# The bias of the first expert layer moved from TensorE to DVE, in the tail of a MetaFormer block

## The chip, the cores and the metric

The kernel runs on one core of one Trainium2 chip. The metric is the device time of one execution in microseconds, as the median of several runs. The engines are named as in the profile: PE (TensorE), DVE (VectorE), ACT (ScalarE), POOL (GpSimd) and SP (SyncE). Each has its own queue of instructions, worked off in order, and the engines meet only through semaphores.

## The reference, cut to what matters

The input is x of 16 batches x 128 x 128 x 128 in float32. A channel attention block with its normalisations comes first. Then follows a layer of 64 experts in which each expert picks its own 8 tokens of each batch:

```python
probs = softmax(t_normed @ gate_w.T + gate_b, axis=tokens)
vals, idx = top_k(probs, 8)                     # per batch and expert
pooled = einsum('bked,bke->bed', x[idx], vals)  # 16 batches x 64 experts x 128
h = gelu(concat(pooled, 1) @ weight1)           # weight1[e]: 129 x 512, row 128 is the bias
out = concat(h, 1) @ weight2                    # weight2[e]: 513 x 128, row 512 is the bias
outputs.at[idx].add(out * vals)                 # scattered back to the picked tokens
```

## The kernel before, in words

The long first part of the kernel streams the 16 batches through all engines: normalise, Gram matrix, attention, output norm, store to `out`, logits, top 8. It is not touched. What follows it, from about 1951 us of the profiled execution to the end, is the tail: the expert layer. Its 64 experts are worked in 16 groups of 4 (`NG`), and 4 groups make a quarter (`Q`). A loop over `SLOTS` = 23 slots, written out in the same way for PE, ACT and DVE, is a software pipeline: in slot t

- PE runs `layer1(t)`, then `turn2(t-3)`, `outputs(t-7)`, `turn1(t-1)`, `codes(t-6)`, `layer2(t-2)` and `combine(t-7)`. When t is a multiple of 4, `pooling(t//4, 1)` comes ahead of `layer1`, and one slot before that `pooling(.., 0)` comes behind it.
- ACT runs `pooled` (line 621, when t is a multiple of 4), the GELU of group t (L632), the copy of the second layer's result of group t-2 (L637), `scales` (L612 and L615, in slots 1, 2, 5, 6, 9, 10), and the copy of the combined rows of t-7 (L645) into one of four buffers `C`.
- DVE runs the copy `OT` of group t-3 (L1127), the product `V` of t-7 (L1135), the copy `HTs` of t-1 (L1141), `equal(t-6)` (L1100 to L1112), and in slots 1, 2, 5, 6, 9, 10 `prepare` (L1078 to L1091), which waits in its middle for the `scales` of ACT and ends with `FW`, the operand of `pooling`.
- POOL scatters: for each of the 16 groups u, once `C` of u and the indices `idxs` of u are there, four indirect DMAs (L490) add the rows to `out`.

GELU and the two functions of `scales` need different activation tables, so ACT loads a table before each change of function.

`layer1(g)` computes the first layer of 4 experts into one PSUM bank `O[g % 2]` of 128 x 512. Expert i of the group has the partitions 32i to 32i+31, and its 16 batches are the first 16 of them. `biases` (L773) first writes the bias to all 32 partitions: for each expert a product of a column of the identity, broadcast to 32, with the 64 x 512 tile `b1s` of all biases. Then the product of `PT` (16 batches) with the weights (L786) is added to it in PSUM. `layer2` (L804) does the same with 128 columns and `b2s`. A product in the profile is two records, so `biases` of one group is 8 of them.

`PT` is written by `pooled`, once per quarter, from a PSUM bank in the order batch, expert into the order expert, batch. SP issues the weight loads: 8 of 256 KB for each group. The loads of group g, from g = 6 on, wait until `layer2(g-6)` is done.

The tiles of the tail lie over those of the first part: `half` is the odd half of `U`, `spare` is `zT`. ACT's GELU reads PSUM and writes `Hs`, of which there are two.

## Time and profile before

| | us |
|---|---|
| median of 3 runs | 2142.67 (2136.2 to 2142.91) |
| the profiled execution | 2155.56 |
| its span, first to last instruction | 2153.8 |
| granted PE clock, mean over the span | 0.957 |

The profiled execution is 12.9 us (0.6%) over the median of the runs. Its times are used for durations, and differences worked out in it are applied to the median. The engines are all 85% to 90% busy over the span, but this is the first part's doing; the tail has to be read by itself.

### The profile page before, as it was taken

How to read it: one execution, taken by the hardware profiler on the slowest of the kernel's cores; microseconds unless marked ns; L12 is line 12 of the kernel's file. 1: busy time of each engine (PE TensorE's matmuls, PEld its weight loads, DVE VectorE, ACT ScalarE, POOL GpSimd, SP SyncE). 2: the span in 40 equal slices, each digit the busy share in tenths (PEclk: the TensorE clock that was granted, in tenths of full speed). 3: DMA queues.
4: the chain of work that ended last, by engine and by line, in shares of the span. 5: the costliest groups of instructions: out<-in, count | busy, mean ns of one | idle time of the engine just before them, and what ended most of it. 6: DMA issues, size and time to landing. Idle time of an engine off the chain costs nothing.

```text
span 2153.8 us, 42420 instructions
## 1 busy us (share of the span) xinstructions
PE 1873.0 (87%) x11917; PEld 1286.6 (60%) x11917; DVE 1822.8 (85%) x4612; ACT 1882.0 (87%) x5020; POOL 1939.2 (90%) x2068
## 2 busy tenths in 40 slices
PE   6999999999999999999999999999999987636991
PEld 6866666666666666666666666666666643213570
DVE  4689999999999898989899999999999899624670
ACT  6899999999999999999999999999999987743420
POOL 5799999999999999999999999999999999961387
PEclk9999999999999999999999999999999998765995
DMA  5498888887888888888788888888788676694963
GB/s 188 157 262 222 228 223 206 226 229 216 218 218 235 224 227 210 224 231 222 215 216 231 229 224 220 212 229 227 213 222 223 178 182 162 165 263 124 282 104 32
DMA packets 111068, 447.92 MB, mean 208 GB/s; under 512 B 10575, under 2 KB 52404, under 8 KB 61684
## 3 DMA queue, kind: packets, MB, share of 16 engines
q1 hardware_dynamic: 81140, 302.61, 42.9%
q0 software_dynamic: 29696, 142.61, 34.2%
q8 instruction: 98, 1.61, 0.3%
q14 instruction: 134, 1.10, 0.1%
HBM read 306.78 MB, written 138.41 MB: 207 GB/s over the span
## 4 chain that ended last, share of the span: by engine, by line
ACT 38%; POOL 21%; issue 17%; PE 16%; DVE 5%; ACTq 1%; DMA 1%; POOLq 0%; SPq 0%; DVEq 0%
ACT U L553 16%; POOL U L430 8%; POOL U L435 7%; ACT zT L516 6%; ACT UT L510 6%; PE G L747 4%; ACT LTS L580 3%; ACT LTS L525 3%; PE T L729 3%; PE O L680 2%; POOL zn L451 2%; POOL out_dram L490 2%; PE T L736 1%; ACT zn L574 1%; POOL U L442 1%
## 5 line engine op out<-in xcount | busy, mean ns | idle before, releaser
L553 ACT ACTIVATE U<-xa,nA,rA 128x128 f32<-128x128 f32 x1948 | 803.7, 483 | 2.1 <-issue 1.3
L747 PEld LDWEIGHTS G<-UT 128*128 128x128 f32 x4096 | 536.8, 192 | 226.5 <-issue 225.3
L430 POOL TENSOR_TENSOR U<-U,bet 128x512 f32<-128x512 f32 x512 | 651.4, 1272 | 2.2
L435 POOL TENSOR_TENSOR U<-U,rO 128x512 f32<-128x512 f32 x512 | 532.2, 1040 | 20.3 <-ACT rO L533 19.3
L747 PE MATMUL G<-UT 128*128 128x128 f32 x4096 | 542.0, 275 | 0.0
L680 PE MATMUL O<-U,MT 128*128 128x512 f32 x1024 | 529.5, 599 | 3.0 <-DVE U L938 3.0
L451 POOL TENSOR_TENSOR zn<-U,rZ 128x512 f32<-128x512 f32 x414 | 446.6, 1079 | 11.0 <-ACT rZ L564 10.3
L936 DVE BATCH_NORM_STATS2 stO<-O 128x6 f32<-128x256 f32 x1024 | 386.8, 423 | 50.2 <-PE O L680 49.5
L729 PE MATMUL T<-ident,U 128*128 128x128 f32 x2048 | 324.3, 281 | 119.1 <-ACT UT L510 108.6
L729 PEld LDWEIGHTS T<-ident,U 128*128 128x128 f32 x2048 | 224.6, 142 | 318.1 <-issue 314.1
L954 DVE BATCH_NORM_STATS2 stA<-xa 128x6 f32<-128x256 f32 x1024 | 386.8, 426 | 31.8 <-DMA xa<-in_x 28.5
L1033 DVE BATCH_NORM_STATS2 stZ<-U 128x6 f32<-128x256 f32 x1024 | 387.4, 424 | 31.1 <-DMA U<-in_x 31.0
L736 PE MATMUL T<-ident,zn 128*128 128x128 f32 x2048 | 322.1, 281 | 75.3 <-ACT zT L516 45.1
L938 DVE TENSOR_TENSOR U<-O,gam 128x512 f32<-128x512 f32 x512 | 348.3, 680 | 0.0
L516 ACT ACTIVATE zT<-T 128x512 f32<-128x512 f32 x512 | 297.6, 581 | 34.0 <-PE T L736 15.1
L736 PEld LDWEIGHTS T<-ident,zn 128*128 128x128 f32 x2048 | 235.6, 143 | 133.0 <-issue 115.0
L510 ACT ACTIVATE UT<-T 128x512 f32<-128x512 f32 x512 | 296.0, 578 | 10.5 <-PE T L729 8.9
L722 PE MATMUL LT<-zT,gwT 128*64 128x512 f32 x1024 | 284.9, 635 | 1.3 <-ACT LTS L525 1.3
L490 POOL DMA_INDIRECT out_dram<-U,UT x64 | 102.2, 1597 | 84.2 <-DVE UT L1112 59.6
L1044 DVE MAX8 CD<-LTS 128x8 f32<-128x2048 f32 x64 | 146.1, 2283 | 35.2 <-issue 35.2
L680 PEld LDWEIGHTS O<-U,MT 128*128 128x128 f32 x1024 | 156.1, 193 | 3.6 <-DVE U L938 3.6
L525 ACT ACTIVATE LTS<-LT 128x512 f32<-128x512 f32 x256 | 150.3, 587 | 2.2 <-issue 2.2
(151 smaller groups left out, 1655.0 us busy)
## 6 DMA issues: line engine op xcount, KB each, us to landing
xa<-in_x SPq DMA_DIRECT2D x128, 1024.0 KB, 6.3
U<-in_x POOLq DMA_DIRECT2D x128, 1024.0 KB, 10.8
out_dram<-U SPq DMA_DIRECT2D x128, 1024.0 KB, 8.6
U<-in_L_ffn_weight SPq DMA_DIRECT2D x112, 256.0 KB
LTS<-in_L_ffn_weight SPq DMA_DIRECT2D x16, 256.0 KB
xa<-out_dram,UT POOLq DMA_INDIRECT x64
out_dram<-U,UT POOLq DMA_INDIRECT x64
zT<-in_L_ffn_weight SPq DMA_DIRECT2D x1, 128.0 KB
```

What stands on the lines that cost most here:

```text
L430: gp.tensor_tensor(rows(a, i), rows(a, i), bet_b, ALU.add).then_inc(S["gb"], 1)
L435: gp.tensor_tensor(rows(a, i), rows(a, i), rO[:, i // 2 % 2, i % 2 * TI:(i % 2 + 1) * TI].unsqueeze(2).to_broadcast([P, TI, W]), ALU.mult) ...
L451: gp.tensor_tensor(zn[:, i % 2, :].rearrange("p (h w) -> p h w", w=W), rows(a, i), rZ[:, k % 2, i % IC * TI:(i % IC + 1) * TI].unsqueeze(2 ...
L510: sc.activation(UT[:, (a[0] * NI + i) % 3, :], T0[:, :], ACT.Copy).then_inc(S["ut_ready"], 1)
L516: sc.activation(zT[:, (a[0] * NI + i) % 3, :], T1[:, :], ACT.Copy).then_inc(S["zt_ready"], 1)
L553: last = sc.activation(utile(a, i, j), xa[:, k % XR, h * W:(h + 1) * W], ACT.Identity, scale=rA[:, k % 2, h:h + 1], bias=nA[:, k % 2, h:h ...
L680: te.matmul(O[i % NO][:, :], MT[:, a[0] % 2, :], chunk(a, i // IC)[:, o:o + IW], start=True, stop=True).then_inc(S["my"], 1)
L729: last = te.transpose(T0[:, j * W:(j + 1) * W], utile(a, i, j), ident[:, :])
L736: last = te.transpose(T1[:, j * W:(j + 1) * W], zn[:, i % 2, j * W:(j + 1) * W], ident[:, :])
L747: last = te.matmul(G[:, 0:P], v, v, start=(i == 0 and j == 0), stop=(i == NI - 1 and j == TI - 1))
L936: last = ve.bn_stats(stO[:, i // 2 % 2, h:h + 2, :].rearrange("p n s -> p (n s)"), pair(O[i % NO], n))
L1033: last = ve.bn_stats(stZ[:, k % 2, j:j + 2, :].rearrange("p n s -> p (n s)"), pair(chunk(a, k), j // 2))
```

## The change

The first layer's bias no longer comes through PE. `b1s`, one 128 KB load by SP, is gone. ACT's queue issues the biases instead: `bias_rows(g)` is four DMAs for group g, each of which reads the 512 biases of one expert and writes them to the expert's 32 partitions of `B1[:, g % 2, :]` (64 KB written by each). `bias_rows(0)` and `(1)` are issued ahead of the slots, behind the wait for the last stores of the first part; `bias_rows(t + 2)` is issued in slot t, behind the GELU of t. DVE gets one instruction per slot, at the head of the slot: it adds `O[t % 2]` and `B1` into `Hs`. The GELU now works in place on `Hs`. `PT` holds each batch twice, so that the products of both layers write all 32 partitions of an expert: their stationary operand has 32 columns where it had 16. `FW` changes its place with no change of size. The wait of `layer1(g)` for the bank is now for DVE's addition of g-2, no longer for the GELU of g-2.

```diff
--- before.py
+++ after.py
@@ -168,10 +168,10 @@
         OUTs = over(spare, 2, W, at=at_t)
         OT = over(half, 2, NB, P, at=at_h)
         first = over(spare, 4, P, at=at_t)
-        b1s = over(spare, HID, at=at_t, parts=E)
+        B1 = over(half, 2, HID, at=at_h)
         b2s = over(spare, W, at=at_t, parts=E)
-        FW = over(half, 2, NB, EQN, at=at_h)
-        PT = over(half, 2, EQN, NB, at=at_h)
+        FW = over(spare, 2, NB, EQN, at=at_t)
+        PT = over(half, 2, EQN, 2 * NB, at=at_h)
         small, at_s = UT[:, :, :].rearrange("p a n -> p (a n)"), [0]
         picked = hot[:, :, :].rearrange("p a n -> p (a n)")
 
@@ -206,11 +206,11 @@
                  "z_bn z_ln z_r zn zn_act u_pool trz zt_ready lg lt_done seg_v seg_i seg_nm seg_exp "
                  "tick cand cross crossed xv t0 t1 t2 texp rsum tv").split()
         S = {n: sem("s_" + n) for n in names}
-        s_tail = sem("s_tail"); s_prep = sem("s_prep"); s_bias = sem("s_bias")
+        s_tail = sem("s_tail"); s_prep = sem("s_prep"); s_bias = sem("s_bias"); s_b1 = [sem(f"s_b1{i}") for i in range(2)]
         s_rows = [[sem(f"s_rows{q}_{h}") for h in range(2)] for q in range(Q)]
         s_sc = [sem(f"s_sc{i}") for i in range(4)]
         s_w = [sem(f"s_w{i}") for i in range(WR // 4)]
-        tnames = ("sel part cut code rowf idx codt codc row eq fst nf idxs rbn rvar rln rr wv cen fw pmm p_done "
+        tnames = ("hb sel part cut code rowf idx codt codc row eq fst nf idxs rbn rvar rln rr wv cen fw pmm p_done "
                   "h ge trh ht o ou tro ott xt v cmm c").split()
         R_ = {n: sem("r_" + n) for n in tnames}
 
@@ -349,7 +349,6 @@
                 weights(e)
 
             sp.wait_ge(S["lg"], NB * NI // 2)
-            sp.dma_start(b1s, w1[:, W, :]).then_inc(s_bias, 16)
             sp.dma_start(b2s, w2[:, HID, :]).then_inc(s_bias, 16)
             sp.wait_ge(S["seg_exp"], NB * NS)
             sp.wait_ge(S["seg_i"], NB * NS)
@@ -618,18 +617,33 @@
                 act.wait_ge(R_["pmm"], 2 * q + 2)
 
                 wait(act, R_["h"], 4 * (q - 1))
-                sc.activation(PT[:, q % 2, :, :].rearrange("p e n -> p n e"),
-                              T0[:, 0:NB * EQN].rearrange("p (n e) -> p n e", e=EQN), ACT.Copy).then_inc(R_["p_done"], 1)
-
+
+                sc.activation(PT[:, q % 2, :, :].rearrange("p e (r n) -> p r n e", n=NB),
+                              T0[:, 0:NB * EQN].rearrange("p (n e) -> p n e", e=EQN).unsqueeze(1).to_broadcast([P, 2, NB, EQN]),
+                              ACT.Copy).then_inc(R_["p_done"], 1)
+
+            def bias_rows(g):
+
+                for i in range(4):
+                    act.dma_start(B1[32 * i:32 * i + 32, g % 2, :],
+                                  w1[4 * g + i:4 * g + i + 1, W, :].to_broadcast([32, HID])).then_inc(s_b1[g % 2], 16)
+
+
+            for k in range(NK):
+                act.wait_ge(s_store[NK + k], 16 * (NB // 2))
+            bias_rows(0)
+            bias_rows(1)
             for h in range(2):
                 scales(0, h)
             for t in range(SLOTS):
                 if t < NG and t % 4 == 0:
                     pooled(t // 4)
                 if t < NG:
-                    act.wait_ge(R_["h"], t + 1)
-                    wait(act, R_["trh"], t - 1)
-                    sc.activation(Hs[:, t % 2, :], O[t % 2][:, :], ACT.Gelu).then_inc(R_["ge"], 1)
+                    act.wait_ge(R_["hb"], t + 1)
+                    sc.activation(Hs[:, t % 2, :], Hs[:, t % 2, :], ACT.Gelu).then_inc(R_["ge"], 1)
+                    if t + 2 < NG:
+
+                        bias_rows(t + 2)
                 if 0 <= t - 2 < NG:
                     g = t - 2
                     act.wait_ge(R_["o"], g + 1)
@@ -777,14 +791,13 @@
                 q = g // 4
                 if g % 4 == 0:
                     pe.wait_ge(R_["p_done"], q + 1)
-                wait(pe, R_["ge"], g - 1)
-                biases(O[g % 2], g, b1s)
+                wait(pe, R_["hb"], g - 1)
 
                 pe.wait_ge(s_w[g % (WR // 4)], 128 * (g // (WR // 4) + 1))
                 for i in range(4):
                     e = 4 * g + i
-                    last = te.matmul(O[g % 2][32 * i:32 * i + NB, :], PT[:, q % 2, e % EQN, :], wslot(e)[:, 0, 0:HID],
-                                     start=False, stop=True)
+                    last = te.matmul(O[g % 2][32 * i:32 * i + 32, :], PT[:, q % 2, e % EQN, :], wslot(e)[:, 0, 0:HID],
+                                     start=True, stop=True)
                 last.then_inc(R_["h"], 1)
 
             def turn1(g):
@@ -801,7 +814,7 @@
                 for c in range(HC):
                     for i in range(4):
                         e = 4 * g + i
-                        last = te.matmul(O[2][32 * i:32 * i + NB, 0:W], HTs[:, g % 2, c * P + 32 * i:c * P + 32 * i + NB],
+                        last = te.matmul(O[2][32 * i:32 * i + 32, 0:W], HTs[:, g % 2, c * P + 32 * i:c * P + 32 * i + 32],
                                          wslot(e)[:, 0, HID + c * W:HID + (c + 1) * W], start=False, stop=(c == HC - 1))
                 last.then_inc(R_["o"], 1)
 
@@ -837,7 +850,7 @@
                                      start=True, stop=True)
                 last.then_inc(R_["cmm"], 1)
 
-            pe.wait_ge(s_bias, 32)
+            pe.wait_ge(s_bias, 16)
             for t in range(SLOTS):
                 if t == 0:
                     pooling(0, 0)
@@ -1117,6 +1130,12 @@
             for h in range(2):
                 prepare(0, h)
             for t in range(SLOTS):
+                if t < NG:
+                    dve.wait_ge(R_["h"], t + 1)
+                    dve.wait_ge(s_b1[t % 2], 64 * (t // 2 + 1))
+
+                    wait(dve, R_["trh"], t - 1)
+                    ve.tensor_tensor(Hs[:, t % 2, :], O[t % 2][:, :], B1[:, t % 2, :], ALU.add).then_inc(R_["hb"], 1)
                 if 0 <= t - 3 < NG:
                     g = t - 3
                     q = g // 4
```

## Rows read from the trace of the kernel before

**Rows 1.** Page, busy time of each engine over the span

```profile
PE 1873.0 (87%) x11917; PEld 1286.6 (60%) x11917; DVE 1822.8 (85%) x4612; ACT 1882.0 (87%) x5020; POOL 1939.2 (90%) x2068
```

**Rows 2.** Stretches: start:end, length, busy by engine, PE clock, DMA share, GB/s

```profile
2100.00:2154.00 54.00, 5.52 (x26) 4.69 (x24) 3.86 (x9) 1.79 (x3) 39.63 (x26) 0.58 0.36 31
```

**Rows 3.** Timeline of POOL: start, us, line, operation, idle before it

```profile
2020.51 1.65 POOL L490 DMA_INDIRECT out_dram<-U,UT  x1 [59.63 <-DVE UT L1112]
...
2030.89 1.56 POOL L490 DMA_INDIRECT out_dram<-U,UT  x1 [3.11 <-ACT U L645]
...
2034.62 1.94 POOL L490 DMA_INDIRECT out_dram<-U,UT  x1 [0.30 <-issue]
...
2040.93 1.56 POOL L490 DMA_INDIRECT out_dram<-U,UT  x1 [2.51 <-ACT U L645]
...
2049.19 1.56 POOL L490 DMA_INDIRECT out_dram<-U,UT  x1 [0.64 <-issue]
...
2145.69 1.56 POOL L490 DMA_INDIRECT out_dram<-U,UT  x1 [0.31 <-issue]
```

**Rows 4.** Of line L490: duration ns min/median/max, first and last start

```profile
L490 POOL DMA_INDIRECT out_dram<-U,UT x64: 1557/1563/2067, 2020.5 to 2145.7; - x64
```

**Rows 5.** Timeline, PE: first layer's bias (L773) and product (L786)

```profile
1967.03 1.93 PE L773 MATMUL O<-zT,ident 64*32 64x512 f32 x8 [0.69 <-ACT U L621]
...
2054.24 1.06 PE L773 MATMUL O<-zT,ident 64*32 64x512 f32 x8 [0.69 <-ACT U L621]
...
2055.24 1.05 PE L786 MATMUL O<-U 128*16 128x512 f32 x8
```

**Rows 6.** Timeline, PE: second layer's bias behind DVE

```profile
1985.81 0.65 PE L773 MATMUL O<-zT,ident 64*32 64x128 f32 x8 [2.07 <-DVE U L1127]
...
2002.70 0.42 PE L773 MATMUL O<-zT,ident 64*32 64x128 f32 x8 [0.44 <-DVE U L1127]
...
2008.78 0.42 PE L773 MATMUL O<-zT,ident 64*32 64x128 f32 x8 [0.91 <-DVE U L1127]
...
2016.32 0.42 PE L773 MATMUL O<-zT,ident 64*32 64x128 f32 x8 [0.15 <-DVE U L1127]
```

**Rows 7.** Timeline, ACT: the pooled copy and the second layer's copy

```profile
1966.38 0.60 ACT L621 ACTIVATE U<-T 128x256 f32<-128x256 f32 x1 [5.02 <-PE T L767]
...
2028.46 0.28 ACT L637 ACTIVATE zT<-O 128x128 f32<-128x128 f32 x1 [4.30 <-PE O L804]
```

**Rows 8.** Timeline, ACT: scales of slot 9, the copy behind

```profile
2035.56 1.28 ACT L612 ACT_TABLE_LOAD   x1
...
2037.94 0.21 ACT L612 ACTIVATE UT<-UT 128x8 f32<-128x8 f32 x1 [1.10 <-issue]
...
2039.58 0.58 ACT L645 ACTIVATE U<-MB 128x512 f32<-128x512 f32 x1
```

**Rows 9.** Timeline, DVE in slot 9 and at the start of slot 10

```profile
2033.71 0.69 DVE L1100 TENSOR_TENSOR U<-G,UT 128x512 f32<-128x512 f32 x1
...
2034.43 0.69 DVE L1106 TENSOR_TENSOR zT<-U,zn 128x512 f32<-128x512 f32 x1
...
2036.16 1.41 DVE L1078 BATCH_NORM_STATS2 zn<-xa 128x6 f32<-128x256 f32 x4
...
2040.12 0.68 DVE L1127 COPY U<-O 128x512 f32<-128x512 f32 x1
```

**Rows 10.** Timeline, SP: issues of weight loads

```profile
2007.01 1.89 SPq L335 DMA_DIRECT2D U<-in_L_ffn_weight  x1
...
2029.31 0.50 SPq L335 DMA_DIRECT2D U<-in_L_ffn_weight  x1
```

**Rows 11.** Stretches of the tail, columns as in the second group

```profile
1966.00:1975.00 9.00, 8.31 (x37) 1.50 (x38) 0.00 (x0) 2.92 (x4) 0.00 (x0) 0.50 0.01 2
...
1985.00:1998.00 13.00, 11.48 (x85) 6.38 (x85) 2.37 (x5) 2.91 (x5) 0.00 (x0) 0.51 0.74 229
...
2010.00:2022.00 12.00, 11.16 (x129) 7.87 (x121) 8.85 (x20) 6.61 (x10) 1.49 (x1) 1.00 1.07 328
```

## The prediction

> **What bounds the kernel now.** I read the first part of the profile's page first: every engine is busy 85% to 90% of the span [rows 1]. That is the first part of the kernel, which the change leaves alone; only the tail can move. The stretches come next: in the last 54 us PE works 5.5, DVE 3.9, ACT 1.8 and POOL 39.6 us [rows 2]. So the end belongs to POOL's scatters. There are 64, of 1.56 us in the median and 0.30 between two, a pitch of 1.87 us [rows 4, 3]. From 2049.19 (first scatter of group u=3) to 2145.69 (the last) are 96.5 us for 51 pitches, 1.89 each: POOL never waits there. It waits only ahead of u=0 (2020.51), u=1 (idle 3.11), u=2 (2.51) and u=3 (0.64), the first for DVE's indices and the others for ACT's copy C [rows 3]. What PE, DVE and ACT do after slot 10 costs nothing: POOL needs 4 x 1.87 = 7.5 us a slot, and the others need less. The end is the latest of: readiness of u, plus 64-4u pitches. So the question is when u=0 to u=3 become ready, and those are made in slots 0 to 10, from 1966 to 2049.
>
> In these slots three chains take turns. In slots 1 to 3 and 5 to 7 it is DVE's prepare, which waits for ACT's scales and their table loads, and keeps PE's second layer waiting for the copy OT: four such waits, before 1985.81, 2002.70, 2008.78 and 2016.32 [rows 6]. In slots 4 and 8 PE itself with the pooled copy. In slots 9 and 10 DVE again: it begins prepare at 2036.16, leaves it at 2040.12 [rows 9], and C of u=2 stands on ACT's queue behind the scales that prepare feeds (2039.58) [rows 8].
>
> **The change part by part.** *PE's bias products go.* Eight records of L773 take 1.93 us at the low clock and 1.06 at the high one, against 1.05 for the product behind them; in a row that is 0.99 us of pitch at the high clock (2054.24 to 2055.24), 1.9 at the low one [rows 5]. The low clock (0.50 granted, 1.2 GHz) holds from 1966 to 1975 and again for nearly all of 1985 to 1998 [rows 11]. Removed: 16 times, of which groups 0, 1 and 4 at 1.9 and 2, 3, 5 to 10 at 1.0. Only where PE is what is late does it count: slots 0, 4, 8, 9.
>
> *DVE's addition comes.* It reads PSUM and SBUF over 128x512, as L1100 does: 0.69 us, about 0.6 from start to start [rows 9]. It stands at the head of DVE's slot, between the product and the GELU. So from the start of layer1 to the GELU 1.9 or 1.0 goes and 0.7 + 0.1 comes. In slots where DVE is late, 0.6 us is added whole.
>
> *The pooled copy doubles.* L621 takes 0.60 us for 256 elements written with a stride [rows 7]; L645 takes 0.58 for 512 contiguous ones [rows 8] and L637 0.28 for 128 [rows 7], which makes 0.17 fixed and 0.83 ns an element. So the strided write costs twice as much an element, and 512 of them cost 0.17 + 0.85 = 1.03 us; the ends are 0.60 (elements alone count) and 1.20 (all doubles). I take 1.03: +0.43 us in slots 0, 4 and 8, whole, as PE waits for it.
>
> *ACT issues four DMAs a slot.* No DMA is issued by ACT before. SP's issues take 0.50 us with quiet engines (2029.31) and up to 1.89 with full ones (2007.01) [rows 10]. The ends are 0 and 4 x 1.89 = 7.6 us a slot; I take four times 0.48, that is 1.9 us, because the quiet row is the kind met in most slots. The eight issues ahead of the slots fall into ACT's idle time before 1957.7 and cost nothing. The others stand between the GELU and the copy L637, where ACT mostly waits for layer2 anyway (4.30 us at 2028.46 [rows 7]): free in slots 4 and 7 to 10. In slots 1 and 2, where GELU and scales follow closely, they cost 1.9 us each.
>
> *The transfers.* 256 KB more a group beside 2 MB of weights; the DMA engines are full from 2010 to 2022 (share 1.07, 328 GB/s [rows 11]), so +12% there, about 0.8 us a group. Each bias has from the GELU of t to the product of t+2, at least 6 us (slot 0 to 2) and mostly 10 to 13. Nothing shown bounds the latency of a second hardware queue; I take it as hidden, with the cost of its failure among the rivals.
>
> *32 columns for 16, 32 rows written, FW's place, b1s gone:* the products stream the same 512 or 128 columns; the weight loads grow inside the pitch. Nothing, at most 0.1 us a slot, hidden behind POOL from slot 11 on.
>
> **The replay.** With these prices and the measured durations of all other instructions I walk the queues from 1966.38, keeping the clock as it was. Slot 0: PT ready +0.4; the product of group 0 ends at 1969.3 instead of 1970.8; GELU of 0 at 1970.1 (before 1970.9). Slots 1 and 2: DVE reaches prepare 3.3 us earlier; the first scales end 1.5 earlier (1977.9), as ACT issues DMAs first; the second scales, another 1.9 later, end at 1984.9 against 1984.5, and DVE now has two additions before its copy: layer2(1) starts at 1986.8 (before 1985.8), 1.0 late. Slot 4: +0.4 for PT, -1.9 for the bias: the product of group 4 ends at 1995.8 (before 1996.3). Slot 5: layer2(3) 2001.6 (2002.7), as the bias of group 5 is gone too. Slot 6: the addition of group 6 stands behind prepare: layer2(4) 2008.5 (2008.8). Slot 7: another addition: layer2(5) 2016.75 (2016.3). So the indices and C of u=0 come 0.45 late, first scatter 2020.95. Slot 8: +0.4 PT, -1.0 bias, and PE, not DVE, is late: C of u=1 ends 1.3 earlier, scatter 2029.6 (2030.9). Slot 9: a second bias gone, DVE enters prepare 2.0 earlier: scatter of u=2 2038.95 (2040.9). Slot 10: DVE is late from here, addition and prepare in a row: u=3 at 2047.9 (2049.2). From there POOL runs through as before. Sum: -1.3 us at u=3, and -1.3 at the end. The bound on the good side: with u=1 to 3 never waited for, POOL would win 0.3 to 5.4 us of gaps [rows 3] and lose the 0.45.
>
> One rule speaks to a term I set to nothing. The scatters of 1.94 us instead of 1.56 start 0.2 us after DVE's L1106, with two SBUF operands (2034.43 and 2034.62 [rows 9, 3]); beside L1100, with one in PSUM, none is long. The addition is of L1100's kind, so I charge nothing; were it of the other, up to 13 collisions of 0.38 us after u=3 would add 5 us. The Trainium skill, "SBUF — State Buffer", section "Who interferes with whom", says that a DVE instruction with two SBUF inputs blocks a GpSimd instruction that reads SBUF and one with at most one does not; by that rule, too, the addition costs POOL nothing, and the two rows fit it.
>
> **The rivals.** *R1, the issues on ACT are slow.* Where the DMA engines are full, SP's issues take twice the quiet time on average and up to 1.89 us. At 1.0 us each in slots 5 to 10, ACT's four take 4.0: scales of slot 5 +2.1, of slot 6 another +2.1, C of u=0 about +4; slots 8 to 10 hide part; u=3 3 to 7 us later than in my replay, so +2 to +6 us: 2144.5 to 2148.5. For it: row 2007.01. Against: these lengthen when SP's own backlog of several groups is long, and ACT has only 4 small transfers at a time. It decides from about 0.8 us an issue.
>
> *R2, the clock.* The change takes work out of PE in slots 1 to 8, and the low clock is already granted after gaps (idle of 2.07 us at 1985.81, then 0.51 over 1985 to 1998 [rows 6, 11]). If it stays low through slots 5 to 8 as well, each has some 3 us of PE work more, half of it on the chain: +6 us, less 1.3: +5, 2147.5. Against: after the change PE still works 7 of 10 us from 1987 to 1998.
>
> *R3, issues cost ACT nothing.* If an issue overlaps the running GELU and is short, slots 1 and 2 win back 3 us, and u=0 to u=3 follow: -4.3, 2138.4. This is the good end and still below 0.3%.
>
> *R4, biases land late.* If the second queue waits behind SP's backlog (2 groups, 4 MB at 328 GB/s, 13 us), DVE waits up to some 3 us in slots 7 to 9 with all its queue behind: +3 to +8 us, 2147. The Trainium skill, "DMA: Bandwidth & Descriptors", section "Queues, rings and completion order", says that each DMA engine goes round robin between its queues by packet; by that rule R4 is out, and no row here shows two hardware queues at once.
>
> *R5, nothing.* The gains and losses cancel, 0: inside the forecast's range.
>
> **How the numbers follow.** The forecast, -1.3 +- 3 us on the median, is 2142.67 - 1.3 = 2141.4. Chances: forecast with R5 0.58, R1 0.14, R2 0.08, R3 0.11, R4 0.05, unforeseen 0.04. Three runs of before spread over 6.7 us, and 0.3% (6.4 us) is about what can be told from no change. Faster by more needs R3 plus the gaps of POOL or a lucky median: 0.10. Slower by more: the upper half of R1, R2 and R4 and a share of the unforeseen: 0.17. Same: 0.73. The range, 2135.5 to 2149.5, holds the forecast, R3 and R1.
>
> **What would show it.** In the changed kernel's profile: L773 at 512 columns gone; the addition 0.69 us, GELU start about 0.8 after the product's end; pooled copy 1.03; ACT's issues about 0.48 apart and no wait of DVE for the biases; the first scatters of u=0, 1, 2, 3 at +0.45, -1.3, -2.0 and -1.3 against those of before, taken from the pooled copy of quarter 0; then 64-12 = 52 scatters in 98 us without a gap. It is wrong if POOL waits in the middle of its run, if ACT's issues exceed 0.8 us, or if the low clock reaches beyond slot 4.

## The result: 0.3% slower

Twelve runs of each kernel on one chip: 2145.88 us in the median after (2140.84 to 2147.94), 2139.54 before (2135.40 to 2142.91). The ratio is 1.0028, 95% interval 1.0018 to 1.0037. Forecast was a gain of 1.3 us; measured is a loss of 6.3. That 2145.88 lies inside the forecast's range of 2135.5 to 2149.5 is no merit of the reasoning: it went the other way.

The profiled execution of the changed kernel took 2147.94 us, its span 2146.2. Busy times hardly move against [rows 1]; the page shows 128 matmuls fewer (8 in each of 16 groups) and ACT's new queue, with 4.20 MB in 0.7% of the DMA engines' time:

```profile
PE 1873.6 (87%) x11789; PEld 1297.7 (60%) x11789; DVE 1832.4 (85%) x4628; ACT 1884.5 (88%) x5020; POOL 1939.1 (90%) x2068
...
q10 hardware_dynamic: 3072, 4.20, 0.7%
```

The two profiled executions reach the tail at different times (the first pooled copy starts at 1966.38 before, at 1951.91 after). That gap is not the change's: on chips where the kernel before takes some 2157 us every version had this copy at 1963 to 1970, where it takes 2139 at 1949 to 1952. So all that follows is measured from the start of the first pooled copy, as the prediction asked. The scatters of u=0, 1, 2, 3, the longest wait after them, and the last scatter; timeline of POOL (start, us, line, operation, idle before it), which answers to [rows 3]:

```profile
2012.28 1.65 POOL L489 DMA_INDIRECT out_dram<-U,UT  x1 [69.09 <-issue]
...
2022.22 1.56 POOL L489 DMA_INDIRECT out_dram<-U,UT  x1 [2.67 <-ACT U L659]
...
2031.37 1.56 POOL L489 DMA_INDIRECT out_dram<-U,UT  x1 [2.00 <-ACT U L659]
...
2040.13 1.56 POOL L489 DMA_INDIRECT out_dram<-U,UT  x1 [1.60 <-ACT U L659]
...
2056.22 1.56 POOL L489 DMA_INDIRECT out_dram<-U,UT  x1 [0.97 <-ACT U L659]
...
2138.02 1.56 POOL L489 DMA_INDIRECT out_dram<-U,UT  x1 [0.30 <-issue]
```

From 1951.91 these are 60.37, 70.31, 79.46, 88.22 and, for the last, 186.11 us. Before they were 54.13, 64.51, 74.55, 82.81 and 179.31. So u=0 to u=3 come 6.2, 5.8, 4.9 and 5.4 us later where the forecast had +0.45, -1.3, -2.0 and -1.3. From u=3 to the end POOL loses another 1.4: 0.67 in the gap ahead of 2056.22, and 0.73 in scatters beside DVE's L1119 (below). Nearly everything is lost before u=0. Two of the prediction's own signs of being wrong are there: POOL waits in the middle of its run (0.97 us ahead of 2056.22), and the low clock reaches beyond slot 4, as the next rows show.

Where? PE's timeline, the second layer's bias of slots 3 and 6 and what runs behind the latter, to be read beside [rows 6]:

```profile
1970.88 0.65 PE L787 MATMUL O<-zT,ident 64*32 64x128 f32 x8 [3.73 <-DVE U L1146]
...
1994.41 0.65 PE L787 MATMUL O<-zT,ident 64*32 64x128 f32 x8 [3.01 <-DVE U L1146]
...
1996.69 1.93 PE L799 MATMUL O<-U 128*32 128x512 f32 x8
...
1998.56 3.60 PE L781 MATMUL T<-zT,xa 128*128 128x16 f32 x16
```

In slot 6 PE waited 0.91 us ahead of this bias before, and now 3.01; in slot 3 it waited 2.07 and now 3.73. And what runs behind the wait is slow: the first layer's product of group 7 (L799) takes 1.93 us, in [rows 5] 1.05. The stretches ahead of the wait, at its end and behind it (columns as in [rows 2]) say so outright:

```profile
1988.00:1991.00 3.00, 2.94 (x43) 1.86 (x36) 2.29 (x5) 1.75 (x3) 0.00 (x0) 1.00 0.94 289
...
1994.00:1996.00 2.00, 1.59 (x28) 1.17 (x32) 1.90 (x4) 0.48 (x1) 0.00 (x0) 0.50 1.11 309
...
1996.00:2008.00 12.00, 12.00 (x97) 9.24 (x93) 8.79 (x19) 5.17 (x7) 0.00 (x0) 0.50 1.12 307
...
2011.00:2020.00 9.00, 7.88 (x81) 5.73 (x81) 4.17 (x7) 2.12 (x4) 6.36 (x4) 0.81 0.92 249
```

Ahead of the wait the grant is 1.00; by its end it is 0.50, that is 1.2 of TensorE's 2.4 GHz. In stretches of 1 us it falls at some 1993.6 and rises at some 2010.7, 17 us later, and from 1994.41 to the rise PE is busy without a break: PE has become what everything waits for. (The fourth row's 0.81 holds a second fall, behind a wait of 1.12 us for the pooled copy of slot 8.) Before, the 12 us that answer to the third row (44 to 56 behind the pooled copy) had 1.00 [rows 11, third row]. This is the prediction's rival R2, with chance 0.08, price +5 us.

### The profile page after: what moved, and what is told of

The parts are those of the page before. It is cut to its first block, busy times and chain, and to the rows that moved or that the text cites. A ratio compares the mean times of both kernels' runs of the same rounds, so it can differ in the third digit from the quotient of the medians.

```text
span 2146.2 us, 42261 instructions
## 1 busy us (share of the span) xinstructions
PE 1873.6 (87%) x11789; PEld 1297.7 (60%) x11789; DVE 1832.4 (85%) x4628; ACT 1884.5 (88%) x5020; POOL 1939.1 (90%) x2068
## 4 chain that ended last, share of the span: by engine, by line
ACT 41%; POOL 21%; PE 16%; issue 15%; DVE 3%; DMA 1%; ACTq 1%; POOLq 0%; SPq 0%; DVEq 0%
ACT U L552 16%; POOL U L429 8%; POOL U L434 7%; ACT zT L515 7%; ACT UT L509 6%; PE G L761 4%; ACT LTS L579 3%; ACT LTS L524 3%; PE T L743 3%; PE O L694 2%; POOL zn L450 2%; ACT zn L573 2%; POOL out_dram L489 2%; PE T L750 2%; PE LT L736 1%
```

## The experiments

The kernel before was timed beside each group of variants on the same chip; chips differ (before takes 2157 us on one, 2138 on another), so a ratio is always to before on the same chip. "Clock" is the mean granted over the whole execution, averaged over a kernel's runs.

**One part of the change at a time.** Four kernels on one chip, before at 2157.58 us, clock 0.9555.

`e1_dup`: the doubled pooled copy and the 32 columns on the kernel before, PE's bias products kept.

```
-        PT = over(half, 2, EQN, NB, at=at_h)
+        PT = over(half, 2, EQN, 2 * NB, at=at_h)
...
+                              T0[:, 0:NB * EQN].rearrange("p (n e) -> p n e", e=EQN).unsqueeze(1).to_broadcast([P, 2, NB, EQN]),
```

> The kernel before, with one part of the change: PT holds each batch twice (the pooled copy has 512 elements) and the products of both layers have 32 columns. The bias stays with PE. Theory A (PE's clock: the change takes work from PE, its waits for DVE grow together, and the clock falls to 0.5 in slots 6 to 8): this part takes no work from PE, so +1.3 us at most (three copies of +0.43 us on the chain), clock unchanged. Theory B (the eight bias transfers ahead of the slots delay the last gather): no transfer is added, so also 0 to +1.3. Theory C (the longer copy and the addition in the chains make the loss): +1 to +2 us of the 6 here.

Measured 2158.5, ratio 0.9999 (0.9986 to 1.0012). The longer copy and the wider products cost nothing that can be seen; in its profile the clock is 1.00 at 44 to 56 us.

`e2_dma`: all bias transfers by ACT on the kernel before, where nobody reads them.

```
+                    if t + 2 < NG:
+                        bias_rows(t + 2)
```

> The kernel before, with all bias transfers issued by ACT as in the changed kernel but read by nobody: PE still adds the bias, GELU reads PSUM, PT single. Theory B (transfers and issues: the ones ahead of the slots delay the last gather by 3.5 us, ACT's issues delay scales): +3 to +6 us. Theory A (clock): PE keeps its work, so 0 to +1.5 us from issues in slots 1 and 2. In the profile B shows DVE waiting for the gather ahead of the second prepare.

Measured 2160.2, ratio 1.0001 (0.9986 to 1.0015). The transfers and their issues alone cost nothing that can be told. Its profiled execution was one of its longest (2164.21), and shows that the clock falls without the change to PE's work, too. Behind a wait of 0.69 us for the pooled copy of slot 8 (PE's bias product at 2023.71) it is 0.50 for 17 us, all of which PE is busy:

```profile
2024.00:2041.00 17.00, 17.00 (x105) 8.75 (x98) 5.36 (x10) 2.07 (x4) 8.52 (x7) 0.50 1.13 320
```

Its last scatter comes 184.62 us behind the pooled copy, 5.3 later than before.

`e3_add`: the changed kernel without the 56 transfers of the slots. The biases of groups 0 and 1 are added to all groups.

```
-                    if t + 2 < NG:
-                        bias_rows(t + 2)
...
-                    dve.wait_ge(s_b1[t % 2], 64 * (t // 2 + 1))
+                    dve.wait_ge(s_b1[t % 2], 64)
```

> The changed kernel without the 56 transfers that ACT issues in the slots: only those of groups 0 and 1 ahead of them are kept, and later groups add those again (the wrong bias). Theory A (clock): the slot transfers are not the cause, the clock still falls to 0.5 in slots 6 to 8 and the time is within 2 us of the changed kernel, +4 to +7 against before. Theory B in its form 'issues and traffic in the slots': the loss goes, within 1.5 us of before. Theory B in its form 'the eight ahead of the slots': +3 to +4 is left.

Measured 2159.67, ratio 0.9998 (0.9986 to 1.0010).

`e4_nobias`: the first layer's bias left out altogether, on PE and on DVE; GELU reads PSUM.

```
-                biases(O[g % 2], g, b1s)
...
-                                     start=False, stop=True)
+                                     start=True, stop=True)
```

> The first layer's bias is left out altogether: no PE products for it, no transfer, no addition by DVE, GELU reads PSUM; PT is doubled. It measures what taking the work from PE brings by itself. If PE's work alone counted, the replay gives -3 to -5 us (1.9 us in slots 0 and 4, 1 us in slots 8 and 9, less 1.3 for the copy). Theory A: PE's waits for DVE in slots 2 to 7 grow by what was taken, the clock falls for longer, and the gain shrinks or turns: -1 to +4 us, with a lower mean clock than before. Theory B or C: -2 to -5, since their costs are all absent.

Measured 2152.79, ratio 0.9966 (0.9952 to 0.9980). With the products gone and nothing in their place the kernel gains 0.34%: the most that moving the bias off PE could bring with PE's waits left bare (the clock dips here too, see below). PE's wait ahead of the second layer in slot 6, in `e3_add` and then in `e4_nobias`:

```profile
2007.70 0.42 PE L784 MATMUL O<-zT,ident 64*32 64x128 f32 x8 [2.61 <-DVE U L1143]
```

```profile
2001.31 0.42 PE L773 MATMUL O<-zT,ident 64*32 64x128 f32 x8 [2.02 <-DVE U L1126]
```

It was 0.91 before [rows 6]; here it is 2.61 with the addition and 2.02 without it. Read against 0.91, the 1.1 us more in `e4_nobias` are the 1.0 us of products taken from PE ahead of the wait, and the 0.6 more in `e3_add` the addition on DVE. The clock at 44 to 56 us: 0.50 and 0.67 in the two halves in `e3_add`, 1.00 and 0.57 in `e4_nobias`.

**The same kernel again, and against the clock.** Four kernels on one chip, before at 2138.11, clock 0.9595.

`e5_after`: the changed kernel, unaltered.

> The changed kernel once more, unaltered, beside the others of this call. Of the chip the two results so far leave open whether the loss is in the tail of every execution. Theory A (clock): a loss of 3 to 7 us against before on any chip, the clock at 0.5 for some 10 us about slots 6 to 8. Theory B (the eight transfers ahead of the slots meet the weight loads and delay the last gather): 6 us where the first part ends early and weights still flow, and only 0 to 3 us where it ends late; its profile shows or lacks DVE's wait for the gather of 3.5 us.

Measured 2145.99, ratio 1.0035 (1.0021 to 1.0049): the loss is confirmed, with clock 0.9538. Its profiled execution happened to be its fastest, 2139.89. There u=0, u=3 and the last scatter start at

```profile
2005.73 1.65 POOL L489 DMA_INDIRECT out_dram<-U,UT  x1 [62.50 <-DVE UT L1125]
...
2033.39 1.56 POOL L489 DMA_INDIRECT out_dram<-U,UT  x1 [1.59 <-ACT U L659]
...
2130.04 1.56 POOL L489 DMA_INDIRECT out_dram<-U,UT  x1 [0.30 <-issue]
```

From the pooled copy at 1951.76 these are 53.97, 81.63 and 178.28 us, so -0.2, -1.2 and -1.0 against before, where the forecast has +0.45, -1.3 and -1.3: the same program, and the forecast's numbers nearly met. PE's wait in slot 6, and the stretches at its end and behind it:

```profile
1993.39 0.65 PE L787 MATMUL O<-zT,ident 64*32 64x128 f32 x8 [2.62 <-DVE U L1146]
```

```profile
1994.00:1996.00 2.00, 2.00 (x39) 1.75 (x40) 1.83 (x4) 0.03 (x1) 0.00 (x0) 0.50 1.12 322
...
1996.00:2008.00 12.00, 10.40 (x113) 7.66 (x105) 8.12 (x19) 7.05 (x10) 1.97 (x2) 0.93 1.12 298
```

Here too the clock falls behind the wait (0.50 from 1994 to 1996), but it is back after 3 us, where it took 17 in the execution above: 0.93 instead of 0.50 from 1996 to 2008. Two executions of one kernel, 8.05 us apart in their times and 7.83 in their last scatters. At the start of this bias they are 0.9 apart (42.50 and 41.63 us behind the pooled copy), at u=0 6.4: they part at this place, by the clock. That is the most direct sight of the cause.

`e6_late`: the first eight bias transfers moved behind the first two scales.

```
-            bias_rows(0)
-            bias_rows(1)
             for h in range(2):
                 scales(0, h)
+            bias_rows(0)
+            bias_rows(1)
```

> The changed kernel with the first eight bias transfers issued behind the first two scales, not ahead of them, so they cannot meet the last gather. Theory B: 3 us faster than the changed kernel where that one shows the wait for the gather, the same elsewhere. Theory A: within 1.5 us of the changed kernel.

Measured 2144.82, ratio 1.0022 (1.0012 to 1.0033), clock 0.9538. Of the eight early transfers 0.1% may come, but the intervals overlap. A trace of it is seen: DVE's second prepare waits for its gathered rows; idle before it and its cause, in the changed kernel and then in `e8_before_warm`, which has no such transfers:

```profile
1945.07 1.42 DVE L1091 BATCH_NORM_STATS2 zn<-xa 128x6 f32<-128x256 f32 x4 [3.54 <-DMA xa<-out_dram,UT]
```

```profile
1942.61 1.43 DVE L1088 BATCH_NORM_STATS2 zn<-xa 128x6 f32<-128x256 f32 x4 [2.68 <-DMA xa<-out_dram,UT]
```

3.54 against 2.68 us; 3.35 in `e5_after` and 2.74 in `e6_late`. So the transfers take some 0.8 us of the gathers' time, ahead of the pooled copy.

`e7_warm`: the changed kernel with products on constants, whose result nobody reads, in PE's waits: 7 ahead of the second layer in slot 3, 6 in slot 6, 4 in slot 9, and 3 ahead of the pooling of slot 3.

```
+            def warm(n):
+                if n:
+                    pe.wait_ge(S["crossed"], NB)
+                for _ in range(n):
+                    te.matmul(MB[:, 0:2 * W], ident[:, :], pick[:, :, :].rearrange("p g n -> p (g n)"), start=True, stop=True)
...
+                warm({3: 7, 6: 6, 9: 4}.get(g + 2, 0))
```

> The changed kernel with products that nobody reads on PE (128x256 of constants into bank MB, 0.43 us each at the high clock) where PE waits for DVE: 3 ahead of pooling(1,0) and 7 ahead of layer2 in slot 3, 6 in slot 6, 4 in slot 9. Theory A: the clock holds at 1.0 from slot 3 to 9 and the scatters start 5 to 9 us earlier than in the changed kernel, so 5 to 9 us less time, at or below before. Theory B or C: the fillers only add to PE's queue, 0 to +3 us against the changed kernel.

Measured 2139.05, ratio 1.0002 (0.9993 to 1.0012), clock 0.9587: the whole loss is won back by adding work to PE. PE ahead of slot 6's second layer (L814 are the added products, two records each, 12 for the 6), there, and in slot 7:

```profile
1987.44 2.86 PE L814 MATMUL MB<-pick,ident 128*128 128x256 f32 x12
...
1990.23 0.42 PE L787 MATMUL O<-zT,ident 64*32 64x128 f32 x8
...
1991.47 1.04 PE L799 MATMUL O<-U 128*32 128x512 f32 x8
...
1998.26 0.42 PE L787 MATMUL O<-zT,ident 64*32 64x128 f32 x8 [1.75 <-DVE U L1156]
...
2001.74 3.43 PE L781 MATMUL T<-zT,xa 128*128 128x16 f32 x16
```

Slot 6's wait is filled, and the product behind it takes 1.04 us instead of 1.93. But now the clock falls one slot later, behind a wait of 1.75 us that stood bare in slot 7: the pooling takes 3.43. Since slots 3 to 6 were faster, u=0 comes at 52.15 all the same.

`e8_before_warm`: the same on the kernel before, 4 in slot 3 and 2 in slot 6.

> The kernel before with the same kind of fillers: 4 ahead of layer2 in slot 3 and 2 in slot 6. Theory A says that before, too, loses time to the low clock behind its wait of 2.07 us in slot 3 (0.5 from slot 3 to 4): 3 to 6 us faster than before. Theory B or C: no change, or up to 1 us slower.

Measured 2140.04, ratio 1.0001 (0.9990 to 1.0011). In its profile u=0 comes 3.0 us earlier than before (51.15), and then the clock is at 0.50 from 52 to 69 us, behind a wait of 0.69 us for the pooled copy of slot 8; u=3 is 3.2 late (86.04). What is gained early is given back.

**Both waits filled.** Three kernels on one chip, before at 2139.31, clock 0.9590.

`e9_warm2`: the changed kernel with such products ahead of the second layer in slots 3, 5, 6, 7, 9, 10 (7, 1, 6, 4, 2, 3 of them), 3 ahead of the pooling of slot 3, and 2 between the second pooling and the wait for the pooled copy in slots 4, 8, 12.

```
+                warm({3: 7, 5: 1, 6: 6, 7: 4, 9: 2, 10: 3}.get(g + 2, 0))
...
                     pooling(t // 4, 1)
+                    warm_lt({4: 2, 8: 2, 12: 2}.get(t, 0))
```

> The changed kernel with more of the fillers (products of constants that nobody reads, into MB or LT): as in the first such kernel, and 1 in slot 5, 4 in slot 7 ahead of layer2, 2 in slots 9 and 3 in 10, and 2 behind pooling(q,1) in slots 4, 8 and 12, where PE waits for the pooled copy. Theory A (clock): the dips left at slots 7 to 8 and 12 go as well, the scatters of u=3 start 2 to 4 us earlier than with the first fillers: 2 to 6 us less than before. If the clock has nothing to do with it: 0 to 3 us slower than the changed kernel.

Measured 2132.84, ratio 0.9973 (0.9962 to 0.9984), clock 0.9635: faster than both kernels.

`e11_before_warm2`: the kernel before with 4 in slot 3, 2 in slot 6 and 1 behind the second pooling in slots 4, 8, 12.

> The kernel before with fillers in slots 3 (4), 6 (2) and one behind pooling(q,1) in slots 4, 8 and 12, where the kernel with fillers in slots 3 and 6 alone had the clock at 0.5 (50 to 68 us behind the first pooled copy). Theory A: that dip goes, 3 to 6 us faster than before. If one product more does not hold the clock: same as before, with the dip in place.

Measured 2135.08, ratio 0.9981 (0.9972 to 0.9990), clock 0.9618. So the cure helps the kernel before too, and with it on both sides the change itself is worth 0.9973 against 0.9981, 1.7 us. It fits the forecast's -1.3, but is not shown: the intervals overlap, and the two kernels have different numbers of added products.

`e10_keepwork`: the changed kernel with PE's bias products kept, on constants; the real product overwrites them. DVE's addition stays.

```
                 wait(pe, R_["hb"], g - 1)
+                biases(O[g % 2], g, ident[0:E, :].unsqueeze(1).to_broadcast([E, 4, P]), stop=True)
```

> The changed kernel in which PE still does the first layer's bias products, on constants, and the real product overwrites them: DVE's addition, ACT's transfers and the doubled copy are all there, only PE's work is not taken. Theory A1 (the clock falls because work was taken from PE): the clock holds at 1.0 where the changed kernel has 0.5 (44 to 56 us behind the first pooled copy), and the kernel is no slower than the changed one, between -5 and 0 us against it. Theory A2 (the clock falls because the addition and the transfers lengthen the chain through DVE and ACT): the clock falls all the same and the kernel is 2 to 5 us slower than the changed one.

Measured 2162.3, ratio 1.0108 (1.0092 to 1.0125), runs from 2144.56 to 2164.46, clock 0.9526. This went against my expectation that PE's work alone keeps the clock. Its profiled execution was the shortest of its five, and has 1.00 from 35 to 79 us, so at 44 to 56 too; the long ones were not profiled. Even this one has its last scatter at 183.28 us, 4.0 later than before, and that much is there by slot 6: its second layer starts at 46.40 us behind the pooled copy, before at 42.40. So beside kept products the rest of the change costs something in this profile without any fall of the clock behind slot 6.

**On the slower kind of chip.** `e12_slot6`, `e13_keepwork_again` beside before at 2155.77 (clock 0.9552), then `e14_after_again`, `e15_slot6_again`, `e16_warm2_again` beside before at 2155.03 (0.9547).

`e12_slot6` and `e15_slot6_again`: the changed kernel with 6 such products in slot 6 alone, `warm({6: 6}.get(g + 2, 0))`.

> The changed kernel with fillers in one place alone: 6 products of 128x256 ahead of layer2 in slot 6, where PE waits 3.0 us for DVE and the clock falls behind it. If that one wait decides (theory A, narrow): 4 to 7 us less than the changed kernel, so within 2 us of before, and the first scatter about 54 us behind the first pooled copy as in the execution that kept the clock. If the earlier waits (slots 3 and 4) matter as much: only 1 to 3 us less, and the clock may fall a little later instead.

> The changed kernel with fillers in slot 6 alone, beside the changed kernel on one chip. Theory A, narrow: 3 to 7 us less than the changed kernel. If the earlier waits matter as much: 0 to 3 us less.

Measured 2157.47, 1.0006 (0.9993 to 1.0019), and 2157.25, 1.0011 (0.9998 to 1.0024). In both profiles the clock holds through slot 6 and then falls one slot later, for some 3 us, behind bare waits of 1.74 and 1.75 us in slot 7, as in `e7_warm`; the last scatter is still 3.3 and 2.4 us later than before.

`e14_after_again`: the changed kernel, unaltered.

> The changed kernel again, in one call with the two below, because the runs so far were on chips of two kinds: on one the kernel before takes about 2138 us and its first part ends near 1934 in the trace, on the other about 2157 and 1951, and the changed kernel was timed on the first kind alone. Theory A: +4 to +8 us against before on either kind, with the clock at 0.5 behind slot 6. If the loss needs the first kind (gather late, weights still flowing): +4 to +8 there and -1 to +3 on the second.

Measured 2160.19, 1.0007 (0.9991 to 1.0024); single runs of either kernel spread over 13 us here, the medians are 5.2 us apart, and the loss is not resolved. Its clock is lower than before's all the same, 0.9511 against 0.9547. Its profiled execution (2161.16) is a third one of the changed kernel, and its low clock lies elsewhere. Behind slot 6's wait of 2.62 us it is low for some 3 us only, as in `e5_after`, and u=0 comes at 53.69, 0.4 ahead of before. But behind a wait of 1.11 us in slot 8 it is at 0.50 for 10 us. POOL waits 4.88 us ahead of u=1, where it had waited 3.11, and later 3.97 ahead of u=5; the last scatter is at 184.34, 5.0 late:

```profile
2022.00:2033.00 11.00, 11.00 (x81) 7.11 (x73) 5.00 (x9) 1.51 (x3) 5.20 (x5) 0.54 1.15 316
```

```profile
2032.77 1.56 POOL L489 DMA_INDIRECT out_dram<-U,UT  x1 [4.88 <-ACT U L659]
...
2070.28 1.56 POOL L489 DMA_INDIRECT out_dram<-U,UT  x1 [3.97 <-ACT U L659]
...
2151.26 1.56 POOL L489 DMA_INDIRECT out_dram<-U,UT  x1 [0.30 <-issue]
```

So the place of the loss changes from execution to execution. Slot 6's products alone bring nothing that can be told: the narrow theory, that this one wait is all, has no support on this chip.

`e13_keepwork_again`: `e10_keepwork` once more.

> The changed kernel with PE's bias products kept on constants, once more: the profile of the first such run was its fastest execution, with the clock held at 1.0 from 44 to 56 us, while most others were some 20 us slower at a lower mean clock. This run is for a profile of such a slow one. Theory A2 (longer chain through DVE and ACT): the clock at 0.5 in more of the 100 us behind the first pooled copy than in the changed kernel. Otherwise (the slow ones differ in the first part of the kernel): the tail is within 3 us of the first profile's and the first part longer.

Measured 2172.28, 1.0074 (1.0050 to 1.0097). Now the profile is of a long execution (2177.81). Stretches of it:

```profile
2012.00:2016.00 4.00, 3.73 (x52) 1.39 (x56) 3.79 (x10) 1.90 (x3) 0.00 (x0) 0.69 1.10 326
...
2016.00:2032.00 16.00, 16.00 (x103) 13.19 (x95) 7.41 (x15) 4.49 (x7) 0.89 (x1) 0.50 0.99 264
...
2036.00:2048.00 12.00, 12.00 (x85) 7.19 (x81) 5.01 (x9) 1.51 (x3) 2.52 (x3) 0.50 0.52 99
...
2052.00:2056.00 4.00, 4.00 (x63) 2.58 (x61) 3.59 (x9) 1.37 (x2) 2.41 (x2) 1.00 0.93 153
```

The clock is 0.50 for some 38 us (2013.5 to 2051.1, 85 us behind the pooled copy), and but for one wait of 1.12 us at 2032.66 PE is busy all the time, 16.00 of 16.00 and 12.00 of 12.00. So more work for PE is no cure in itself: here the clock fell behind a wait of 1.49 us, in slot 6, and with a low clock the kept products make the loss larger. In the profile of `e10_keepwork` the same wait of the same program is as long, and the clock stays at 1.00. The two waits, there and then here:

```profile
1997.86 0.42 PE L787 MATMUL O<-zT,ident 64*32 64x128 f32 x8 [1.49 <-DVE U L1147]
```

```profile
2012.27 0.42 PE L787 MATMUL O<-zT,ident 64*32 64x128 f32 x8 [1.49 <-DVE U L1147]
```

They start 46.40 and 46.44 us behind the pooled copy. The wait's length alone does not decide.

`e16_warm2_again`: `e9_warm2` once more.

> The changed kernel with fillers in slots 3 to 12, again, beside the changed kernel on one chip: 10 to 14 us less than it, 5 to 8 less than before, and the clock at 1.0 from 32 us behind the first pooled copy on.

Measured 2147.86, 0.9962 (0.9947 to 0.9977), clock 0.9593, its nine runs within 4.7 us where before's 26 spread over 13. The stretches at 44 to 56 us and behind them, then u=0, u=3 and the last scatter:

```profile
2009.00:2021.00 12.00, 11.81 (x147) 9.02 (x145) 8.69 (x16) 3.89 (x7) 5.80 (x4) 1.00 1.13 314
...
2021.00:2055.00 34.00, 32.38 (x359) 23.42 (x358) 26.99 (x58) 16.52 (x25) 25.15 (x17) 1.00 1.17 312
```

```profile
2014.28 1.65 POOL L489 DMA_INDIRECT out_dram<-U,UT  x1 [54.36 <-DVE UT L1142]
...
2041.03 1.56 POOL L489 DMA_INDIRECT out_dram<-U,UT  x1 [1.59 <-ACT U L659]
...
2137.58 1.56 POOL L489 DMA_INDIRECT out_dram<-U,UT  x1 [0.30 <-issue]
```

From the pooled copy at 1965.42 that is 48.86, 75.61 and 172.16 us: 7.2 us ahead of before at the last scatter, as the times have it (7.17). The cure gains about as much on this kind of chip as on the other (0.27% there, 0.38% here).

## Why the prediction was wrong

The step that failed is the sentence "I walk the queues from 1966.38, keeping the clock as it was", with the rival against it, R2, at a chance of 0.08. In its place the clock stood at 0.50 for 17 us behind slot 6's wait, and u=0 came 6.2 us late. The other terms of the sum:

- *The replay:* its numbers are met by `e5_after`'s profile: -0.2, -0.8, -1.7, -1.2 at u=0 to u=3 and -1.0 at the end, forecast +0.45, -1.3, -2.0, -1.3, -1.3. In part that is luck. The clock was not kept there either: it was low from 14 to 34 us behind the pooled copy, where before it had been from 19 to 33, and once more for 3 us in slot 6. Against that, the second layer of slot 3 starts at 18.6 us and not at the replay's 20.4, in the main because ACT's issues were priced too high (below). The two errors about cancel by slot 5 (34.95 us, replay 35.2).
- *The pooled copy:* 1.03 us, as worked out from [rows 7, 8]. *The addition:* 0.69, as said, and 0.6 from start to start where a copy follows, though the two rows named for it in [rows 9] are 0.72 apart. In DVE's timeline:

```profile
1955.00 0.69 DVE L1138 TENSOR_TENSOR U<-O,U 128x512 f32<-128x512 f32 x1 [6.77 <-PE O L799]
```

- *The biases' arrival (R4):* DVE never waited for them. Issue to landing is 4.9 us in the median (page of `e5_after`) beside the weights. The Trainium skill, "DMA: Bandwidth & Descriptors", section "Queues, rings and completion order", says that each DMA engine takes turns between its queues. The trace agrees as far as these 4.9 us go, against the 13 of R4's backlog; that the gathers' 0.8 us are the other side of the same turns is argued, not shown.
- *ACT's issues (R1, R3):* priced too high, but not free as R3 had it. In ACT's timeline the pooled copy, the GELU of slot 0 and the four issues behind it; the table load of slot 1's scales; the first issue of slot 2 and its GELU; the second layer's copy behind them; and the costliest group, in slot 5:

```profile
1951.91 1.03 ACT L621 ACTIVATE U<-T 128x512 f32<-128x512 f32 x1 [4.74 <-PE T L781]
...
1955.72 0.63 ACT L643 ACTIVATE U<-U 128x512 f32<-128x512 f32 x1 [1.48 <-DVE U L1138]
...
1955.73 1.73 ACTq L628 DMA_DIRECT2D U<-in_L_ffn_weight  x4
...
1959.38 1.28 ACT L611 ACT_TABLE_LOAD   x1 [1.24 <-issue]
...
1963.57 0.32 ACTq L628 DMA_DIRECT2D U<-in_L_ffn_weight  x1
...
1963.72 0.63 ACT L643 ACTIVATE U<-U 128x512 f32<-128x512 f32 x1
...
1965.69 0.28 ACT L651 ACTIVATE zT<-O 128x128 f32<-128x128 f32 x1 [1.35 <-issue]
...
1986.49 2.62 ACTq L628 DMA_DIRECT2D U<-in_L_ffn_weight  x4
```

Four take 1.73 us, 0.43 each, but they start at 1955.73, 0.01 us after the GELU of 0.63 has started, not behind it; the issue at 1963.57 even ran before the table load ahead of the GELU at 1963.72 had ended. What stands behind the four waits for them: 1.24 us in slot 1 and 1.35 in slot 2, where the replay had 1.9 each. With full DMA engines four took 2.62, 0.65 each, below R1's 0.8 in the mean; single issues reached 1.27 in this profile, 0.64 in `e5_after`, with a median of 0.44 in both. `e2_dma` can't tell all of them together from nothing.
- *R2, the clock:* price near (+5 forecast, +6.3 measured), place wrong: I looked at slots 5 and 4, where the low clock already stood, and asked whether it would stay. It did go up again, and fell anew behind slot 6's wait. The chance of 0.08 was too small, and the replay held what would have raised it. It has layer2(3) at 2001.6 and layer2(4) at 2008.5, 6.9 us apart. Between the two PE works 2008.78 - 0.91 - 2002.70 = 5.2 us [rows 6], 4.2 without the bias products: a gap of 2.7 us (measured: 3.01) where there had been 0.91, and [rows 6, 11] show the clock at 0.51 behind the gap of 2.07. I added up when PE is late and didn't hold my own gaps against the one that had cost the clock.

Two things had worked against each other there. The bias products gone made PE early, and the additions on DVE made the copy late. The replay had both, but the wait between them was taken as free, since PE was "not late".

What is shown, first: of four profiled executions, three of the changed kernel and one of `e6_late`, the two whose clock stays low at 44 to 56 us behind the pooled copy are 6.8 and 7.3 us late at the last scatter (the first profile and `e6_late`), one whose clock comes back is 1.0 early (`e5_after`), and one whose clock comes back there but falls for 10 us in slot 8 is 5.0 late (`e14_after_again`). Second: work that does nothing, put into PE's waits, gives the loss back (`e7_warm`) and more (`e9_warm2`, `e16_warm2_again`). Third, and weaker: the parts alone cost nothing that can be told (`e1_dup`, `e2_dma`, `e3_add`). These three ran on the slower kind of chip only, where the whole change costs 0.07% and can't be told from nothing either.

What isn't settled: how much of the fall is due to the work taken away and how much to the wait made longer. `e1_dup` (work kept, no addition) keeps 1.00, `e4_nobias` (work gone, no addition) dips in part, `e10_keepwork` and `e13_keepwork_again` (work kept, addition) have it both ways, behind waits of equal length. What decides between executions stays open. Nor is it settled why the loss of 0.3% on one kind of chip is only 0.07%, unresolved, on the other; the kernel before is the more scattered there (13 us against 8), and may lose the clock itself in some executions, which would leave less to lose. I have no long profile of it, but `e2_dma` and `e8_before_warm`, which keep all its work on PE, show such a fall, 17 us behind a wait of 0.69 in slot 8, and the profile of before itself has one there of some 3 us (2022.9 to 2026.3).

## What to carry to other kernels

A wait of an engine off the critical path is not free when the engine is TensorE: list its waits before and after a change, and where one grows to the length of one behind which the profile already shows a low grant, price a stretch behind it at the lower clock (3 to 38 us here), as one case among several, for single executions differ. A change that takes work off PE should come with a look at whether something useful, or failing that something useless, fills the wait: here that was worth 0.27 to 0.38% with the change, against the 0.06% forecast for the change itself; and it took several waits, for filling one alone (`e12_slot6`) moved the fall to the next. And where single executions of one kernel differ by several us, profile it more than once: here the pair showed the cause, and a third profile that the place varies.

## What the runs showed of the hardware

- The granted clock fell to 0.50 behind waits of 0.69 us (for the pooled copy of slot 8: before, `e2_dma`, `e8_before_warm`) to 4.1 us (slot 3, `e13_keepwork_again`), not behind each of them and not in each execution of one kernel. How long it stayed there varied as much. With PE busy without a pause it was 3 us in `e5_after` and 17 in the first profile, `e2_dma` and `e8_before_warm`; with one wait of 1.12 us between, 10 in `e7_warm` and some 38 in `e13_keepwork_again`.
- A DMA issue on ACT takes 0.44 us in the median, four in a row 1.73, and runs beside an activation or a table load that has started; the next instruction of ACT waits for the rest (1.24 and 1.35 us above).
- The long scatters behind 2049 go with one DVE instruction. The longest in the changed kernel's run, and the DVE instruction that had just started, in POOL's and DVE's timelines:

```profile
2074.88 2.07 POOL L489 DMA_INDIRECT out_dram<-U,UT  x1 [0.30 <-issue]
```

```profile
2074.82 0.69 DVE L1119 TENSOR_TENSOR zT<-U,zn 128x512 f32<-128x512 f32 x1
```

All six scatters of over 1.6 us behind 2049, and all five before, start within 0.6 us behind the start of this multiplication, which reads two SBUF operands; none beside the new addition, with one operand in PSUM. (Ahead of 2049 the first scatter of either kernel, 1.65 us, and one of 1.63 at 2046.92 before are long without it.) Six cost 2.04 us over the median, five had cost 1.31: the 0.73 of the result. The Trainium skill, "SBUF — State Buffer", section "Who interferes with whom", says that a DVE instruction with two SBUF inputs contends with a GpSimd instruction that reads SBUF, and one with at most one SBUF input, outside the 2-port modes, does not; these scatters agree, and the prediction's nothing for the addition stood.
